# A four-stage decoder layer on one core: one block for all stages, tensors at fixed places, and each stage's first tile and weights prepared in the last tile of the stage ahead

## The reference, cut to what matters

```
x = layernorm(x + mixer_and_mlp(x))        # stages 1 and 2
x = layernorm(x + cross_attention(x, ctx)) # stage 3, 16 heads of 32, 256 keys
x = layernorm(x + quantised_ffn(x))        # stage 4, 512 -> 2048 -> 512

mixer_and_mlp:  h = x + mamba2_mixer(rmsnorm(x));  return h + down(silu(gate(u)) * up(u)),  u = rmsnorm(h)
mamba2_mixer:   in_proj 512 -> 2320, causal conv of 4, scan with state 128, 16 heads of 64, rmsnorm, out_proj 1024 -> 512
quantised_ffn:  relu(x @ w1.T + b1) rounded to 4+3 bits, times w2 rounded the same way, plus b2, rounded
```

## Time and profile before

| | |
|---|---|
| median of 3 runs | 2943.56 us (2943.02 to 2945.01) |
| the profiled execution, its own time | 2944.89 us |
| span of the profile | 2943.1 us |
| PE busy | 2748.9 us, 93% of the span |
| DVE, ACT, POOL busy | 1561.0, 1031.7, 570.2 us |
| DMA | 148.01 MB, mean 50 GB/s |

### The profile page before, as it was taken

How to read it: one execution, slowest core, us unless ns; L and a number is a source line. 1 busy time by engine, 2 the same in 40 slices (tenths; PEclk the granted TensorE clock), 3 DMA queues, 4 the chain that set the end, 5 groups by cost and what they waited for, 6 DMA issues and landing times. The chain is left out here.

```text
span 2943.1 us, 42150 instructions
## 1 busy us (share of the span) xinstructions
PE 2748.9 (93%) x15200; PEld 2101.7 (71%) x15200; DVE 1561.0 (53%) x2603; ACT 1031.7 (35%) x2385; POOL 570.2 (19%) x532
## 2 busy tenths in 40 slices
PE   6999999999979999999999689999999968999998
PEld 4777777777757777877778467766777746777765
DVE  6787788788764231222212377777777752211122
ACT  6244334424424222212221255545455434222221
POOL 0543453364340100101000011122121110000000
PEclk9999999999989999999999799999999988999999
DMA  3011101101013110111011220111101015121111
GB/s 128 20 39 43 43 0 43 43 1 42 29 63 126 58 53 4 57 57 57 11 46 43 101 76 9 51 57 57 57 7 57 29 44 162 44 85 43 43 43 43
DMA packets 85273, 148.01 MB, mean 50 GB/s; under 512 B 3824, under 2 KB 17776, under 8 KB 85200
## 3 DMA queue, kind: packets, MB, share of 16 engines
q1 hardware_dynamic: 85200, 147.03, 14.5%
HBM read 113.46 MB, written 33.55 MB: 50 GB/s over the span
## 5 line engine op out<-in xcount | busy, mean ns | idle before, releaser
L1214 ACT ACTIVATE at_pr<-at_sc,at_nm 128x256 f32<-128x256 f32 x512 | 237.3, 481 | 222.2 <-DVE at_nm L1375 222.2
L960 DVE TENSOR_TENSOR gm_m_lo<-gm_m,gm_m_hi 128x512 fp32r<-128x512 f32 (+1 forms) x88 | 60.8, 691 | 426.2 <-ACT gm_m_hi L887 426.2
L72 PE MATMUL gm_ps<-gm_u_hi,gm_gu_hi 128*128 128x512 f32 (+1 forms) x704 | 279.3, 397 | 4.2 <-DVE gm_gu_lo L157 4.2
L73 PE MATMUL gm_ps<-gm_u_lo,gm_gu_hi 128*128 128x512 f32 (+1 forms) x704 | 280.3, 398 | 0.0
L74 PE MATMUL gm_ps<-gm_u_hi,gm_gu_lo 128*128 128x512 f32 (+1 forms) x704 | 278.1, 395 | 0.0
L72 PE MATMUL mx_ps<-mx_u_hi,mx_win_hi 128*128 128x512 f32 (+1 forms) x608 | 245.8, 404 | 14.1 <-DVE mx_xdt L484 5.9
L1381 DVE COPY at_pT<-at_pt 128x512 f32<-128x512 f32 x256 | 176.3, 689 | 125.6 <-PE at_pt L1532 122.1
L73 PE MATMUL mx_ps<-mx_u_lo,mx_win_hi 128*128 128x512 f32 (+1 forms) x608 | 242.0, 398 | 0.0
L74 PE MATMUL mx_ps<-mx_u_hi,mx_win_lo 128*128 128x512 f32 (+1 forms) x608 | 241.4, 397 | 0.0
L881 ACT ACTIVATE gm_sg<-gm_ps 128x512 f32<-128x512 f32 (+1 forms) x88 | 52.6, 597 | 538.2 <-PE gm_ps L74 538.2
L1532 PE MATMUL at_pt<-at_cols,at_pr 128*128 128x128 f32 x1024 | 165.1, 285 | 50.9 <-DVE at_pT L1381 48.4
(11 more groups left out here) (263 smaller groups left out, 6036.6 us busy)
## 6 DMA issues: line engine op xcount, KB each, us to landing
mx_xf<-in_x SPq DMA_DIRECT2D x8, 1024.0 KB, 7.4
mx_xr<-in_x SPq DMA_DIRECT2D x8, 1024.0 KB, 5.9
h_scratch<-mx_xr SPq DMA_DIRECT2D x8, 1024.0 KB, 5.0
gm_hf<-h_scratch SPq DMA_DIRECT2D x8, 1024.0 KB, 8.2
gm_xr<-in_x SPq DMA_DIRECT2D x8, 1024.0 KB, 7.3
gm_r<-h_scratch SPq DMA_DIRECT2D x8, 1024.0 KB, 6.1
x_scratch<-gm_r SPq DMA_DIRECT2D x8, 1024.0 KB, 5.0
at_xf<-x_scratch SPq DMA_DIRECT2D x8, 1024.0 KB, 7.4
```

The source lines that it names most:

```text
L72: nc.tensor.matmul(out, l_hi, r_hi, start=first, stop=False)
L73: nc.tensor.matmul(out, l_hi, r_lo, start=False, stop=False)
L960: V.tensor_tensor(m_lo[j % 2][0:n, :], m[j % 2][0:n, :], m_hi[j % 2][0:n, :].bitcast(F32), ALU.subtract).then_inc(s["ml"], 1)
L1214: A(pr[h][:, t, :], SC[h][:, SEQ * t:SEQ * t + SEQ], ACT.Exp, bias=nm[:, 4 * n + h, t:t + 1], accum_out=sums[:, 2 * b + t, 4 * g + h:4 * g ...
```

## The change

**One block.** `build` opens a single `nc.Block()`; each stage returns its five streams, and each engine runs those of the four stages in a row. No engine meets the others between stages; instead the next stage waits for single semaphores of the one ahead (`prev.s[...]`).

**Fixed places.** Every tensor gets a fixed SBUF offset (`Place`, `SEG`). The stages' tensors lie over each other by a plan, so that each weight, small tensor and staging slot of a next stage that is written early lies where the stage ahead has finished by then. The tile buffers for the front of a tile (`xf`, `u_hi`, `u_lo`), the identity, the epsilons and the norm's small tensors are `Shared` by all four stages, their semaphores counted on from stage to stage (`i + B`, with B = 8, 16, 24). The eight PSUM banks are shared too.

**The last tile of a stage** now does the front of tile 8, which is the next stage's tile 0: SP loads it, ACT and DVE split it, PE turns it. Also there: the next stage's small tensors, the load of its first weights, and their high and low parts: 8 pieces for the gated MLP, 8 for attention (and the context tile), 12 for the quantised MLP.

**Small things.** The identity is an input of its own instead of a part of each stage's columns, which with `post_w` makes two more small DMAs ahead of the first weights. `r_hl` and its transpose cover 32 rows instead of 128. The gated MLP's weights are split into separate tensors in the order of their use. `steps` has no `first` any more.

```diff
-def steps(eng, first, main):
+def steps(eng, main):
 
-    first(0)
-    main(0, True)
+    main(0)
     with eng.Fori(1, NP - 1) as i:
-        main(i, True)
-    main(NP - 1, False)
+        main(i)
+    main(NP - 1)
...
+ROOM = 16384
+SHARED = 25344
+SEG = [ROOM + SHARED + o for o in (0, 41472, 74240, 107008, 115200, 123392, 156160, 172544)]
...
         # mixer, SP
+            sp.dma_start(xf[:, :, :], hs[0] if final(i) else xs[i + 1]).then_inc(s["xf"], 16)
...
+            if final(i):
+
+                sp.wait_ge(s["sl"], NCONV * NP)
+                sp.wait_ge(s["G"], NP)
+                me.nxt.wt.load(sp, 4)
+                sp.wait_ge(s["g"], KI * i + 4)
+                me.nxt.wt.load(sp, 12)
...
         # mixer, ACT
+                if final(i) and j >= 1:
+
+                    me.nxt.wt.high(act, j if j <= 4 else 4 + 2 * max(j - 5, 0))
...
         # mixer, DVE
+                if final(i) and 2 <= j <= 5:
+                    me.nxt.wt.low(dve, j - 1)
+            g_low(i, KI - 1)
+            split(i + 1, 2)
+            split(i + 1, 3)
+            if final(i):
+                me.nxt.wt.low(dve, 8)
+            dve.wait_ge(s["ss"], i + 1)
...
         # gated MLP, SP
+            if final(i):
+                me.nxt.load_small(sp)
+
+                sp.wait_ge(s["hx"], TT * NP)
+                me.nxt.wt.load(sp, 4)
+                sp.wait_ge(s["dn"], KM * i + 2)
+                me.nxt.load_context(sp, 0, 0)
+                me.nxt.load_context(sp, 0, 1)
+                me.nxt.wt.load(sp, 8)
+            sp.wait_ge(s["ln"], TT * i + TT)
+            sp.dma_start(os[i], r[:, :, :]).then_inc(s["st"], 16)
...
         # gated MLP, DVE
+                elif final(i) and 6 <= j <= 9:
+                    me.nxt.wt.low(dve, j - 5)
+            split(i + 1, 2)
+            split(i + 1, 3)
+            if final(i):
+                me.nxt.wt.low(dve, 8)
+            dve.wait_ge(s["dn"], KM * i + KM)
...
         # attention, ACT
+                if not more and n >= 3:
+
+                    act.wait_ge(s["proj"], before(i, 4) + 1)
+                    me.nxt.wt.high(act, min(2 * (n - 2), 12))
...
         # attention, DVE
+                if not more and n == 2:
+                    me.nxt.constants(dve)
+                elif not more and n > 3:
+                    me.nxt.wt.low(dve, min(2 * (n - 3), 12))
```

And in `build`, where four blocks become one:

```diff
-        block = ctx.enter_context(nc.Block())
...
+        block = ctx.enter_context(nc.Block())
...
+            for stage in stages:
+                stage.sync(sp)
```

More of the change, by code:

```diff
@@ L58, in step_0, with final @@
     return isinstance(i, int) and i == 0
-def steps(eng, first, main):
-    first(0)
-    main(0, True)
+def final(i):
+    return isinstance(i, int) and i == NP - 1
+def steps(eng, main):
+    main(0)
     with eng.Fori(1, NP - 1) as i:
-        main(i, True)
-    main(NP - 1, False)
+        main(i)
+    main(NP - 1)
 def mm3(nc, out, l_hi, l_lo, r_hi, r_lo, first, last):
@@ L1850, in sem @@
             return ctx.enter_context(nc.semaphore(name))
-        su = Counts(sem)
+        su, sh = Counts(sem), Shared(nc, sem)
+        ps = [ctx.enter_context(nc.psum_tensor(f"ps{b}", [P, 512], F32)) for b in range(8)]
         h1 = nc.dram_tensor("h1_scratch", (TOK, DM), F32, kind="Internal").ap()
```

2840 lines of the change are left out of this document (1443 added, 1397 removed).

## The result

| | before | after |
|---|---|---|
| median | 2944.28 us of 4 runs (2943.02 to 2947.86) | 2830.66 us of 4 runs (2830.18 to 4476.92) |
| the profiled execution's span | 2943.1 us | 2828.4 us |
| PE busy | 2748.9 us | 2701.0 us |

One of the four runs after was disturbed (TensorE's clock at 0.557 on average, 4476.92 us) and is left out of the ratio.

The account below looks back on a forecast made before the run. The prediction took PE, busy 93%, as the bound, with only the seams between stages to win: 29.7 + 33.4 + 20.4 - 0.5 = 83.0 us off 2943.56, forecast 2860 us, 80% range 2850 to 2874.

Parts of the forecast that it names:

- Seam 1: Mixer to gated MLP: 29.7 us less, including a 2.0 wait for weights' lows; ends 28 and 31.8.
- Seam 2: Gated MLP to attention: 33.4 us less, with ends of 30 and 36.6.
- DVE's takes: Attention's first projections: PE fills four banks, then waits for DVE, still at the gated tail and lows; 1.9 us lost.
- The 1.3 for the late second half of the weights: Attention's start: pieces 9 to 16 load behind the tile's store, 4 to 5 us later, hidden up to 1.3 us.
- The clock, whose 3.4 were to come back whole: Attention's first projections: clock of 0.89 over 31 us loses 3.4 us, all regained because PE hasn't idled.
- Seam 3: Attention to quantised MLP: 20.4 us less, with ends of 17 and 24.
- "3.5" for the lows in attention's last tile with "1 more for a clock": Attention's last tile: weights' lows in pairs on the path cost 3.5 us, a clock low for longer 1 more.
- The start: Kernel start: two more small DMAs ahead of the weights cost 0.5 us, at worst 1.5.
- The step that failed: All tiles: fixed SBUF places cost or give 0, with bounds of 0.1 us a tile, 3 us in all.
- The rival of slower loops: All stages' loops: tiles take over 2.8 us longer, ending above 2949 us; chance 0.3 in 10.
- The rival of the lows lengthened beside POOL: Weights' lows beside POOL's work: 8 of 20 on the path cost 6 us; within late weights, 2 in 10.
- the signs of being wrong: PE wait over 3 us at a seam, clock under 0.9 behind one, gated tile not 94.17, many lows of 1.4 us.

Follow-up runs that it names:

- experiment 4: The changed kernel without the early loading and splitting of the next stage's weights in a last tile: 2870.18 us, ratio 0.9752 to the kernel before.
- experiment 1: The kernel before, with larger SBUF tensors of the mixer, gated and quantised MLP placed at multiples of 256 bytes, attention left: 2919.95 us, ratio 0.9918.
- experiment 2: The changed kernel with the shared tensors (next tile, u_hi, u_lo, identity) moved by 96 bytes: 2854.77 us, ratio 0.9699 to the kernel before.
- experiment 3: Layer left out, PE alone makes products at 64 pairs of operand offsets: 226.7 ns at distance 0 (one pair 227.9), 228.9 at +64, elsewhere 232.4 to 234.3.
- (5): The changed kernel with each row of the mixer's wx weights on a multiple of 256 bytes: 2826.01 us, ratio 0.9595 to the kernel before.

## Why the prediction was wrong where it was

**Seam 1: right, in part by luck.** Forecast 29.7, measured 29.6. PE waited 1.60 for `gu_lo` instead of 2.0, and the clock stayed up. Two errors of 1.2 to 1.4 cancel. The last mixer tile is longer by 1.4 for the early weights (experiment 4), which the forecast put at nothing; and from its sum of squares to the first L1085 are 93.13 (856.26 to 949.39), a steady tile and 0.8, where the forecast had a tile and 2.0. (Its lower end was added up wrongly: 29.7 less 2.8 is 26.9, not 28.)

**Seam 2: right, again with terms that cancel.** Forecast 33.4, measured 32.9. The first q product follows the last down product, and DVE's takes cost the 1.9. The 1.3 for the late second half of the weights did not come as such (0.37 on ACT, hidden). In its place stand 1.6 more of waiting for the first probabilities, 3.16 for 1.55, since DVE, late with the takes, is late with the row maxima too. The clock, whose 3.4 were to come back whole, is at 0.96 over the 26 us from 1600 on.

**Seam 3: the mechanism right, a term too small.** Forecast 20.4, measured 18.8. The term is "3.5" for the lows in attention's last tile with "1 more for a clock": by experiment 4 the early weights cost 5.5, part of it clock, and the late products at the lower clock 1.5 on top (4.35 for 2.9). What the prediction did not count, 0.4 more at the second w1, made up for little of it. The difference of 1.6 to the forecast is smaller than what attention's uneven periods before the change leave open (18.8 or some 21).

**The start: not to be told apart from nothing.** Forecast -0.5; the first sum of squares came at 139.75 instead of 141.18, of which some 0.96 is the shorter tile. But it came at 139.63 with the old start in experiment 1 and at 138.98 with the new one in experiment 4.

**The step that failed** is that of the fixed places: "no row shows that a fixed place in SBUF costs or gives anything, so it stands at 0, with 0.1 us a tile, 3 us in all, as its bounds". The loops gave 34 us, 1.1 a tile, where it allowed for 3. Of the gain the seams are 81 us and were forecast as 83.5; the miss is this term. It was right that no row showed it, and wrong to make of that a bound of 3 us. In a loop where PE is busy for 690.00 of 690.00 us the interval of a product is the whole price, and a changed place is a changed operand of every one of those products. The rival of slower loops even had the right lever (0.229 to 0.236 a product) with the sign against the one that came: the same 7 ns exist, and the kernel before was already paying them.

That the places did it in the mixer, the gated and the quantised MLP is shown by four runs: they give the kernel before 23.6 us without any other change (1), moving them by 96 bytes takes 24.1 of the gain away (2), the interval follows the distance with all else absent (3), and more of it is to be had by aligning more (5). By tiles, 0.65, 1.17 and 1.08 us a tile in experiment 1, 23.2 for 8 tiles each, are measured as places alone, of 31.0 for the three stages. The rest of the three is what the changed kernel's separate tensors align further (0.68 in the gated tile); that attention's 0.53 a tile comes from places as well is argued and was not tried. For it speaks that its 192 products of `wq`, `wk`, `wv` and `wo` in a tile were all at distance 128 and are at 0, with means of 232.4 to 232.7 ns before and 230.2 to 230.8 after (some 0.4 us a tile); against it that in experiment 2 the q products went back to 233.2 ns and the tile did not get longer (88.61).

**The rival of the lows lengthened beside POOL** came for four of the 28 early lows. The Trainium skill, "SBUF — State Buffer", section "Who interferes with whom", has VectorE and GpSimd lock each other out of a shared port pair, and 1.43 beside POOL agreed. DVE and POOL at three places of the changed kernel:

```profile
827.79 0.75 DVE L213 SCALAR_TENSOR_TENSOR gm_gu_lo<-gm_r,sh_post_w,gm_gu_hi 128x512 fp32r<-128x512 f32 x1
...
829.13 1.30 POOL L481 TENSOR_TENSOR mx_acc<-mx_acc,mx_sq 128x512 f32<-128x512 f32 x1 [2.32 <-ACT mx_sq L456]
...
1595.07 2.56 DVE L211 TENSOR_TENSOR at_wk_lo<-at_o,at_wk_hi 128x512 fp32r<-128x512 f32 x2 [0.75 <-ACT at_wk_hi L200]
...
1594.07 3.00 POOL L1287 TENSOR_TENSOR at_c_lo<-at_cf,at_c_hi 128x512 fp32r<-128x512 f32 x2 [13.19 <-ACT at_c_hi L1283]
...
2317.71 2.90 DVE L211 TENSOR_TENSOR qm_w_lo<-qm_stage,qm_w_hi 128x512 fp32r<-128x512 f32 x2
...
2315.90 5.85 POOL L1444 TENSOR_TENSOR at_r<-at_r,at_cols 128x512 f32<-128x512 f32 x4
```

The first low stands where POOL is idle and takes 0.75, as the four between the mixer's scans all do. The two pairs start inside POOL's operations and take 2.56 and 2.90, where a pair alone takes 1.3; in the raw trace each of the four ends 0.55 after the POOL operation in which it began, as `g_lo` did in the earlier trace rows and does in all 40 such places of the changed kernel. Two lows that began inside another POOL operation, L837 on 128x4, kept their 0.68. What it cost is small. Behind the second pair PE is busy with slow products until 2323.85 and does not wait for DVE. Behind the first pair DVE goes on without a pause to the gated tail and the takes, so up to 1.3 of seam 2's waits can be due to it; no run separates that. The 6 us of this rival did not come, because few lows fall beside POOL and fewer are on the path.

The Trainium skill, "SBUF — State Buffer", section "SBUF: two separate sides", says that of the engines only the shared pair causes contention, and that PE never waits on anyone. In experiment 3 no other engine was at work, and still the interval of PE's products differed by up to 7.6 ns with the places of its own two operands. There the measurement decides: PE can be slowed by itself.

**Of the signs of being wrong** that the prediction named, three came: a gated tile of 92.32, which is the failed step; a wait of 3.16 at seam 2; and a clock of 0.82 at seam 3 (2335 to 2341 us). The fourth, lows of 1.4 us in numbers, did not: three of 28 took 1.2 to 1.8.

## What to carry to other kernels

Where the tensor engine is the bound, put the moving and the stationary operand of a product at the same place modulo 256 bytes, row by row (a row length that is no multiple of 256 spoils it for the rows after the first); in the fp32 triples of 512 columns here this is worth up to 3% of the interval, and it costs an alignment argument (fp8 products did not need it). When a change moves tensors, put the interval of the products into the sum with both signs, and measure it by itself on constant data before trusting a loop's steady state. A seam between stages can be priced well from the last undisturbed event to the first one of the next stage, plus what waits next; here three such prices were right within 2 us in their sums, with single terms off by 1 to 3 us.
